# Feed-forward layers on split f32: three rounded products for each full one

## The reference

```python
even, odd = lt[:, ::2, :], lt[:, 1::2, :]          # tokens 1..16 of each batch
m1 = (even[:, :4, :, None] * odd[:, :4, None, :]).reshape(Bx, Hx, Dx)
m2 = (even[:, 4:, :, None] * odd[:, 4:, None, :]).reshape(Bx, Dx, Hx)
h = einsum('bsd,hd->bsh', x, W1) + scale * einsum('bsd,bhd->bsh', x, m1) + b1
h = gelu(h, approximate=False)
out = einsum('bsh,oh->bso', h, W2) + scale * einsum('bsh,boh->bso', h, m2) + b2
...
x = x + 0.5 * ffn(layernorm(x))
```

## Time and profile before

| what | us |
|---|---|
| median of 3 runs | 3112.09 (3107.85 to 3112.73) |
| the profiled execution, its own time | 3102.54 |
| its span | 3100.8 |
| PE busy in the span | 2719.5 (88%) |
| DVE busy | 2029.5 (65%) |
| ACT busy | 1148.7 (37%) |
| POOL busy | 884.5 (29%) |

### The profile page before, as it was taken

How to read it: one execution, slowest core, us unless ns; L and a number is a source line. 1 busy time by engine, 2 the same in 40 slices (tenths; PEclk the granted TensorE clock), 3 DMA queues, 4 the chain that set the end, 5 groups by cost and what they waited for, 6 DMA issues and landing times. The chain is left out here.

```text
span 3100.8 us, 53905 instructions
## 1 busy us (share of the span) xinstructions
PE 2719.5 (88%) x15208; PEld 1879.4 (61%) x15208; DVE 2029.5 (65%) x5166; ACT 1148.7 (37%) x2097; POOL 884.5 (29%) x1200
## 2 busy tenths in 40 slices
PE   6999999958787888789999999768988989889986
PEld 5888888735454555468888887334554554454453
DVE  6777777747776777577777777445555555556533
ACT  3111111126575657521111111324544535545532
POOL 3333223225555555442233222001211111111200
PEclk9999999968888888889999999878999999999988
DMA  3000000000000000020000000000101101101100
GB/s 134 0 0 0 0 0 0 1 1 3 3 2 3 3 3 2 17 84 0 0 0 0 0 0 0 1 23 27 45 24 35 37 25 36 36 24 38 34 1 27
DMA packets 31864, 52.01 MB, mean 17 GB/s; under 512 B 8066, under 2 KB 13954, under 8 KB 31620
## 3 DMA queue, kind: packets, MB, share of 16 engines
q1 hardware_dynamic: 27012, 41.88, 4.3%
q0 software_dynamic: 4608, 7.09, 0.9%
HBM read 17.93 MB, written 2.10 MB: 6 GB/s over the span
## 5 line engine op out<-in xcount | busy, mean ns | idle before, releaser
L603 DVE SCALAR_TENSOR_TENSOR moe_acc<-moe_ps,moe_comb,moe_acc 128x512 f32<-128x512 f32 x896 | 660.4, 743 | 153.1 <-PE moe_ps L310 146.8
L2149 DVE CUSTOM_DVE_ANT_0 attn_masked<-attn_psm,attn_causal 128x256 f32<-128x256 f32 (+7 forms) x512 | 368.6, 756 | 271.3 <-PE attn_psm L1846 270.3
L2051 ACT ACTIVATE attn_probs<-attn_pse 128x512 f32<-128x512 f32 (+1 forms) x640 | 313.2, 556 | 324.9 <-PE attn_pse L1861 322.2
L310 PE MATMUL moe_ps<-moe_Wg,moe_xh 128*128 128x512 f32 x1024 | 328.1, 402 | 17.4 <-DVE moe_Wg L526 17.4
L341 PE MATMUL moe_ps<-moe_Wd,moe_ih 128*128 128x512 f32 x1024 | 339.3, 413 | 4.7 <-DVE moe_Wd L526 4.7
L310 PE MATMUL moe_ps<-moe_Wu,moe_xh 128*128 128x512 f32 x1024 | 332.0, 406 | 3.5 <-POOL moe_Wu L464 3.5
L1769 POOL TENSOR_SCALAR_AFFINE_SELECT attn_probs<-attn_probs 128x256 f32<-128x256 f32 (+1 forms) x192 | 95.0, 495 | 726.3 <-ACT attn_probs L2051 726.3
L1877 PE MATMUL attn_psy<-attn_probs,attn_V 128*64 128x512 f32 (+3 forms) x1536 | 288.7, 506 | 0.0
L474 POOL TENSOR_SCALAR moe_part<-consts,moe_pick,moe_prob 128x8 f32<-128x8 f32 x256 | 97.4, 394 | 626.0 <-ACT moe_prob L398 626.0
L1077 POOL TENSOR_TENSOR attn_R<-attn_R 128x1024 f32<-128x1024 f32 (+1 forms) x128 | 215.0, 1687 | 200.2 <-DVE attn_R L1421 200.1
L1846 PE MATMUL attn_psm<-attn_kS,attn_qS 108*128 108x512 f32 (+3 forms) x672 | 199.0, 397 | 45.7 <-DVE attn_mx L2149 39.7
(11 more groups left out here) (218 smaller groups left out, 4802.5 us busy)
## 6 DMA issues: line engine op xcount, KB each, us to landing
attn_qS<-attn_qH SPq DMA_DIRECT2D x192, 72.0 KB
attn_qS<-attn_qL SPq DMA_DIRECT2D x96, 72.0 KB
attn_qS<-attn_qH POOLq DMA_DIRECT2D x64, 72.0 KB, 2.0
moe_stageg<-in_w_gate SPq DMA_DIRECT2D x8, 512.0 KB, 7.1
moe_stageu<-in_w_up SPq DMA_DIRECT2D x8, 512.0 KB, 7.2
moe_stageg<-in_w_down SPq DMA_DIRECT2D x8, 512.0 KB, 4.4
attn_qS<-attn_qL POOLq DMA_DIRECT2D x32, 72.0 KB, 2.5
out<-X SPq DMA_DIRECT2D x1, 2048.0 KB, 8.7
```

What stands on the lines that cost most here:

```text
L310: last = pe.matmul(expert_bank[j % 4][:, :], a[q][:, :], w[b][:, cols], start=k == 0, stop=k == 2)
L603: dve.scalar_tensor_tensor(acc[:, q, r, :], expert_bank[j % 4][:, :], comb[:, q, r, e:e + 1], acc[:, q, r, :], ALU.mult, ALU.add).then_inc ...
L2051: act.activation(probs[:, ring(q, u), c, HALF - n:HALF], e_part(k, HALF - n, HALF), ACT.Exp, scale=SCORE_SCALE).then_inc(p_ready, 1)
L2149: dve.tensor_tensor_reduce(masked[:, 0 if j >= 4 else 1, 0:n], m_all[:, base:base + n], causal[:, SEQ - n:SEQ], 1.0, NEG, ALU.add, ALU.max ...
```

## The change

Each operand of L796 and L806 (tokens, both weight tiles, inner values) is held twice: a high part, the f32 value rounded to the `float32r` format, and a low part, the difference rounded in its turn. A product of f32 operands becomes three of the rounded format: high by high, and the two mixed ones; low by low is left out. ACT rounds the tokens as it copies them, and in addition the two weight tiles (`high_weights`). POOL rounds the eight tiles of inner values (its new program). DVE makes all low parts: `low_x` from the transposed tokens in PSUM, `low_weights` and `low_hidden` from SBUF. On DVE the next batch's preparation is taken apart, and the low parts are put between its pieces. Pair products and transposes stay as they are.

```diff
--- before.py
+++ after.py
@@ -720,7 +720,7 @@
         first_half, second_half = small[0:8, 8:12], small[0:8, 12:16]
         b2h = sb("b2h", [P, 1])
         xn = sb("xn", [P, BT, DIM])
-        xT = sb("xT", [P, SEQ])
+        xT = [sb(f"xT{i}", [P, SEQ], F32R) for i in range(2)]
         even = sb("even", [8, DIM])
         odd = sb("odd", [8, DIM])
         evens = sb("evens", [8, DIM])
@@ -728,7 +728,11 @@
         evenm = sb("evenm", [8, 4, 4, 32])
         w1e = sb("w1e", [P, INNER])
         w2e = sb("w2e", [P, INNER])
+        w1s = [sb(f"w1s{i}", [P, INNER], F32R) for i in range(2)]
+        w2s = [sb(f"w2s{i}", [P, INNER], F32R) for i in range(2)]
         hid = sb("hid", [P, 2, KC, HALF])
+        hs = [sb(f"hs{i}", [P, 2, KC, HALF], F32R) for i in range(2)]
+        PRODUCTS = ((0, 0), (1, 0), (0, 1))
         oT = sb("oT", [P, 2, HALF])
         res = ResidualAdd(ctx, nc, sem, t, tag, 4)
         ps = [ctx.enter_context(nc.psum_tensor(f"{tag}_ps{i}", [P, HALF], F32)) for i in range(8)]
@@ -739,6 +743,9 @@
         xt_ready, xt_copied, wp_ready, we_ready = sem("xt_ready"), sem("xt_copied"), sem("wp_ready"), sem("we_ready")
         h_ready, hid_ready, o_ready, o_copied = sem("h_ready"), sem("hid_ready"), sem("o_ready"), sem("o_copied")
         ot_ready = sem("ot_ready")
+        xh_ready, wh_ready, wl_ready, hh_ready, hl_ready = (
+            sem("xh_ready"), sem("wh_ready"), sem("wl_ready"), sem("hh_ready"), sem("hl_ready"))
+        pool_pause, dve_pause = sem("pool_pause"), sem("vector_pause")
 
         def pipeline(eng, start, run):
 
@@ -790,20 +797,26 @@
                 def run(b, more):
                     for s in range(2):
                         pe.wait_ge(xt_copied, after(b * 2 + s))
-                        pe.wait_ge(we_ready, after(b * 2))
+                        pe.wait_ge(wl_ready, after(b * 2))
                         for c in range(KC):
                             pe.wait_ge(hid_ready, after((b * 2 + s - 1) * KC + c))
-                            pe.matmul(h_bank[c][:, :], w1e[:, c * P:(c + 1) * P], xT[:, s * HALF:(s + 1) * HALF],
-                                      start=True, stop=True).then_inc(h_ready, 1)
+                            for k, (x, w) in enumerate(PRODUCTS):
+                                last = pe.matmul(h_bank[c][:, :], w1s[w][:, c * P:(c + 1) * P], xT[x][:, s * HALF:(s + 1) * HALF],
+                                                 start=k == 0, stop=k == 2)
+                            last.then_inc(h_ready, 1)
                     if more:
                         transpose_x(b + 1)
                         pair_products(b + 1, 0)
-                    pe.wait_ge(we_ready, after(b * 2 + 1))
+                    pe.wait_ge(wl_ready, after(b * 2 + 1))
                     for s in range(2):
                         pe.wait_ge(o_copied, after(b * 2 + s - 1))
                         for c in range(KC):
-                            pe.wait_ge(hid_ready, after((b * 2 + s) * KC + c))
-                            last = pe.matmul(o_bank[:, :], w2e[:, c * P:(c + 1) * P], hid[:, s, c, :], start=c == 0, stop=c == KC - 1)
+                            pe.wait_ge(hh_ready, after((b * 2 + s) * KC + c))
+                            for k, (h, w) in enumerate(((0, 0), (0, 1), (1, 0))):
+                                if h:
+                                    pe.wait_ge(hl_ready, after((b * 2 + s) * KC + c))
+                                last = pe.matmul(o_bank[:, :], w2s[w][:, c * P:(c + 1) * P], hs[h][:, s, c, :],
+                                                 start=c == 0 and k == 0, stop=c == KC - 1 and k == 2)
                         last.then_inc(o_ready, 1)
                     if more:
                         pair_products(b + 1, 1)
@@ -822,7 +835,7 @@
             @block.scalar
             def _(act):
                 layernorm_scales(act, t, rstd_ready)
-                for s in (xt_copied, hid_ready, o_copied):
+                for s in (xh_ready, wh_ready, hid_ready, o_copied):
                     act.sem_inc(s, LEAD)
                 act.wait_ge(b2h_ready, 1)
 
@@ -830,7 +843,11 @@
                     for s in range(2):
                         act.wait_ge(xt_ready, after(b * 2 + s))
                         act.wait_ge(h_ready, after((b - 1) * 2 * KC + (s + 1) * KC - 1))
-                        act.activation(xT[:, s * HALF:(s + 1) * HALF], x_bank[s][:, :], ACT.Copy).then_inc(xt_copied, 1)
+                        act.activation(xT[0][:, s * HALF:(s + 1) * HALF], x_bank[s][:, :], ACT.Copy).then_inc(xh_ready, 1)
+
+                def high_weights(b, layer):
+                    act.wait_ge(we_ready, after(b * 2 + layer))
+                    act.activation((w2s if layer else w1s)[0][:, :], (w2e if layer else w1e)[:, :], ACT.Copy).then_inc(wh_ready, 1)
 
                 def run(b, more):
                     for s in range(2):
@@ -840,17 +857,38 @@
                             act.activation(hid[:, s, c, :], h_bank[c][:, :], ACT.Gelu, bias=b1[:, c:c + 1]).then_inc(hid_ready, 1)
                     if more:
                         copy_x(b + 1)
+                        high_weights(b + 1, 0)
                     for s in range(2):
                         act.wait_ge(o_ready, after(b * 2 + s))
                         act.wait_ge(ot_ready, after((b - 1) * 2 + s))
                         act.activation(oT[:, s, :], o_bank[:, :], ACT.Identity, bias=b2h[:, :], scale=0.5).then_inc(o_copied, 1)
-
-                pipeline(act, lambda: copy_x(0), run)
+                    if more:
+                        high_weights(b + 1, 1)
+
+                def start():
+                    copy_x(0)
+                    for layer in range(2):
+                        high_weights(0, layer)
+
+                pipeline(act, start, run)
+
+            @block.gpsimd
+            def _(pool):
+                pool.sem_inc(hh_ready, LEAD)
+
+                def run(b, more):
+                    for s in range(2):
+                        for c in range(KC):
+                            pool.wait_ge(hid_ready, after((b * 2 + s) * KC + c))
+                            pool.sem_inc(pool_pause, 1)
+                            pool.tensor_copy(hs[0][:, s, c, :], hid[:, s, c, :]).then_inc(hh_ready, 1)
+
+                pipeline(pool, lambda: None, run)
 
             @block.vector
             def _(dve):
                 layernorm_reciprocals(dve, t, rstd_ready)
-                for s in (xn_ready, pairs_ready, we_ready):
+                for s in (xn_ready, pairs_ready, we_ready, xt_copied, wl_ready, hl_ready):
                     dve.sem_inc(s, LEAD)
                 res.prime(dve)
                 dve.wait_ge(s_in, 16)
@@ -887,20 +925,48 @@
                         dve.wait_ge(o_ready, after(b * 2 - 1))
                         dve.tensor_tensor(w2e[:, :], w_bank[:, :], w2[:, :], ALU.add).then_inc(we_ready, 1)
 
-                def prepare(b):
-                    normalise(b)
-                    pairs(b)
+                def low_weights(b, layer):
+                    w, e = (w2s, w2e) if layer else (w1s, w1e)
+                    dve.wait_ge(wh_ready, after(b * 2 + layer))
+                    dve.tensor_tensor(w[1][:, :], e[:, :], f32(w[0][:, :]), ALU.subtract).then_inc(wl_ready, 1)
+
+                def low_x(b):
+                    for s in range(2):
+                        half = slice(s * HALF, (s + 1) * HALF)
+                        dve.wait_ge(xh_ready, after(b * 2 + s))
+                        dve.tensor_tensor(xT[1][:, half], x_bank[s][:, :], f32(xT[0][:, half]), ALU.subtract).then_inc(xt_copied, 1)
+
+                def low_hidden(b, s):
+                    for c in range(KC):
+                        dve.wait_ge(hh_ready, after((b * 2 + s) * KC + c))
+                        dve.sem_inc(dve_pause, 1)
+                        dve.tensor_tensor(hs[1][:, s, c, :], hid[:, s, c, :], f32(hs[0][:, s, c, :]), ALU.subtract).then_inc(hl_ready, 1)
+
+                def start():
+                    normalise(0)
+                    pairs(0)
+                    low_x(0)
                     for layer in range(2):
-                        element_weights(b, layer)
+                        element_weights(0, layer)
+                        low_weights(0, layer)
 
                 def run(b, more):
                     if more:
-                        prepare(b + 1)
+                        normalise(b + 1)
+                    low_hidden(b, 0)
+                    if more:
+                        pairs(b + 1)
+                    low_hidden(b, 1)
+                    if more:
+                        low_x(b + 1)
+                        for layer in range(2):
+                            element_weights(b + 1, layer)
+                            low_weights(b + 1, layer)
                     for s in range(2):
                         dve.wait_ge(ot_ready, after(b * 2 + s))
                         res.add(dve, b * 2 + s, s, b * BT + 4 * s, x_bank[s][:, :])
```

(2 more changed lines are left out.)

## The result

The changed kernel takes 3134.63 us, median of 4 runs (3129.32 to 3142.34), against 3109.97 for the kernel before (3106.03 to 3112.73, 4 runs): a ratio of 1.0082, 95% interval 1.0055 to 1.0109. Forecast were 3131 us, range 3114 to 3141. Its profiled execution took 3129.32 us, with a span of 3127.5. In what follows PE is also called TensorE, DVE VectorE, ACT ScalarE and POOL GpSimd.

A forecast was written before the change was run, and what follows sets the result against it. The prediction saw no engine alone as the bound, but an alternating chain of waits. Middle batches +10.2, first +9.4, last -1.2 and clears +0.6 gave +19.0 us on 3112.1, so 3131 us, range 3114 to 3141.

The forecast's parts named there:

- The adds behind the low second-layer weights: Middle batch, VectorE: residual adds wait for rounding and subtraction of the second-layer weights, +1.4 us.
- Hidden subtractions ahead of the pairs: Middle batch, VectorE: four subtractions (2.44 us) delay pairs from 10.31 to 13.6, pair products from 12.38 to 15.7.
- 1.2 GHz from the pair products on: Middle batch, TensorE: after idling, pair products take 2.0 us, then 5.5 to the second half; batch 27.3, +2.9.
- bounds +3.0 and +25.8: Four middle batches together: +3.0 us if the clock stays full, +25.8 with second halves at the low clock too.
- First batches: First batch of each phase: POOL's copies and VectorE take turns, +3.5 us; slow clock afterwards, +1.2; +4.7 each.
- Last batches: Last batch of each phase: the second half of the second product saves its 0.63 us; -0.6 each.
- Clearing seven more semaphores: SP, each phase: seven more semaphore clears, from nothing to 0.8 us, taken as 0.3; +0.6 in all.
- no blocking: Rival, 18%: POOL's copies do not stop VectorE, clock low; first batches -1.2 each, +7.2 us, 3119.
- the full clock: Rival, 8%: POOL blocks VectorE but TensorE's clock stays full; middle batches +3.0 us, first +3.1 each, +8.6, 3121.
- TensorE as the bound: Rival, 3%: TensorE bounds the feed-forward phase after all, so cheaper products take 20 us off, 3092.
- Second halves at the low clock: Rival, 5%: second halves of the second product also run at the low clock; past +28 us, 3140 and more.
- A normalise that goes free: First batch: a normalise outside VectorE's two-port mode escapes POOL's lock; turns end 0.6 us sooner, +2.9 for +3.5.

The follow-up runs named there:

- Experiment 1: Changed kernel with VectorE's four first-half hidden subtractions moved behind the pair arithmetic: 3128.0 us, ratio 1.0059 to the kernel before.
- experiment 4: Changed kernel plus six unread full f32 matmuls per batch with a successor, in TensorE's gaps around the next transposes: 3122.0 us, ratio 1.0044 to the kernel before.
- experiments 3: Changed kernel with the high hidden parts made by ScalarE instead of POOL, which has no feed-forward work left: 3127.7 us, ratio 1.0059 to the kernel before.
- experiment 7: Kernel before plus only POOL's eight copies of hidden values per batch, into a tile nobody reads: 3115.8 us, ratio 1.0028.

## Why the prediction was right, and where not

- *The adds behind the low second-layer weights, +1.4:* 2.20 was forecast and is there. The way to the normalising is another 0.3 longer by POOL's turns, which the prediction saw only in first batches.
- *Hidden subtractions ahead of the pairs:* pair products at 15.84 against 15.7. Experiment 1 took this step back: 1.6 us a middle batch.
- *1.2 GHz from the pair products on:* 2.0 and 5.95 us to the second half against 2.0 and 5.5; experiment 4 shows the cause, not only the coincidence. The batch is 27.5 to 27.8 against 27.3, four of them +11.5 against +10.2 (bounds +3.0 and +25.8).
- *First batches:* +2.7 and +3.9, against +4.7 each. The mechanism is there (experiments 3 and 7), its size was too large: copies began 3.9 us after the first product's start, when the normalising (2.58 us) was nearly over, so only four subtractions and the pairs took turns, at 2.4 us. The prediction had counted all eight copies, 4.2 us, in series with VectorE's work. Pair products came 11.7 after that start; by the prediction's sum it would have been 13.0. From there to the output transposes ffn1's first batch took 12.2, a little more than the 11.6 forecast.
- *Last batches, forecast -0.6 each, measured +0.1:* the term that failed. The adds ended at 8.7, not 8.2, held by POOL's copies, which also run here; the subtractions followed at 8.85, and TensorE stood 2.56 us in the middle of the first half. Behind that wait it had ten matmuls still to do, 2.59 us, so the half ended at 12.2, 0.9 after its fourth subtraction and not 0.3; 11.0 was forecast:

```profile
3095.24 5.73 PE L804 MATMUL ffn_ps<-ffn_xT,ffn_w1s 128*128 128x512 f32 x24
...
3100.53 0.87 DVE L122 COPY X<-ffn_xo 128x512 f32 x1
...
3100.81 0.61 PE L818 MATMUL ffn_ps<-ffn_hs,ffn_w2s 128*128 128x512 f32 x2
...
3103.24 4.91 DVE L943 TENSOR_TENSOR ffn_hs<-ffn_hid,ffn_hs 128x512 fp32r<-128x512 f32 x8
...
3103.99 2.59 PE L818 MATMUL ffn_ps<-ffn_hs,ffn_w2s 128*128 128x512 f32 x10 [2.56 <-DVE ffn_hs L943]
```

- *Clearing seven more semaphores, +0.3 a phase:* the time from the last statistics copy to the output's transfer at the end of ffn1, where the clears stand, is 1.47 us in both profiles of before, 1.87 in the changed kernel and 1.59 with the two semaphores of experiment 7: 0.4 a phase, near the forecast.
- *Sum:* +18.3 us in the layers against +18.4 without the clears. First batches were put 2.9 too high, middle and last ones 2.7 too low, so that the sum is better than its terms is luck. The timed medians differ by 24.7; most of the rest is in the attention between, for which the prediction had no term, and whose cause is open. The forecast of 3131 against 3134.6 is close in part because it started from 3112.1 us for the kernel before, where four runs gave 3110.0.
- *Rivals:* no blocking falls by experiments 3 and 7, the full clock by the windows above and experiment 4. TensorE as the bound falls too: the halves at full clock are as cheap as said, 3.02 for 3.70, and the kernel was slower. Second halves at the low clock were not seen: 3.02 in the changed kernel's middle batches, at 1.00.

The Trainium skill, SBUF — State Buffer, section Who interferes with whom, names copies and tensor_scalar in their two-port modes beside instructions with two SBUF inputs as what a GpSimd instruction can shut out. The runs agree: the normalising (2.85 for 2.30), the second copy of the adds (0.68 for 0.43) and the statistics copy were held, while L118, one of whose inputs is PSUM, kept its 0.68 and the batch-norm statistics their 0.86. A normalise that goes free, which the prediction weighed, is not what the rows show.

## What to carry to other kernels

Where a product is made cheaper by splitting its operands, price first where the splitting work stands on the engine that feeds the next product: here the order of one engine's queue was worth 21 us in the layers (209.7 to 188.2), more than the 7 us that separate the two kernels with spare matmuls. Moving one wait shows the next one (pairs, then the output copy behind a rounding on ScalarE, then the clock), so read the timeline after each edit and not only the time. In gaps of TensorE of 0.8 to 3.6 us ahead of the second product, a few matmuls that nobody reads cost nothing here and, in most batches, returned the clock; more of them than the gap held delayed what followed, as in the first batches of experiment 4.

## What was not expected of the hardware

- Four spare matmuls of 0.9 us in the gaps took 2.8 us off a middle batch (24.74 to 21.92), three took 2.0 off one of the kernel before (24.75 to 22.72).
- With one spare matmul between transposes and pair products, the same code kept its clock in one layer (21.9 us) and lost it in the other (23.5).
- A VectorE copy of 8 values per partition, 0.17 us alone, took 0.63 beside POOL's copies of 0.60 each: the turn, not the size, was the price.
- An attention layer that no edit touches took 947 us in both profiles with the unedited layers and 948 to 957 in twelve with edited ones; whether the edits bring this is open.
